# Routing the four-expert layer of a GNN/FFN kernel: dense blocks against blocks of one expert

## What is computed

```python
scores = _layernorm(agg, ln_gamma, ln_beta).reshape(M, HEADS, NUM_EXPERTS).mean(1)
...
topk_s, topk_i = jax.lax.top_k(scores, TOP_K)      # NUM_EXPERTS 4, TOP_K 2
w = jax.nn.softmax(topk_s, axis=-1)
out = jnp.zeros_like(x)
for ei in range(NUM_EXPERTS):
    g = jnp.where(topk_i == ei, w, 0.0).sum(-1)
    hh = jax.nn.gelu(x @ W1[ei] + b1[ei], approximate=False)
    out = out + g[..., None] * (hh @ W2[ei] + b2[ei])
```

## Time and profile before

| | |
|---|---|
| time, median of 3 runs | 7084.68 us (7082.7 to 7098.25) |
| the profiled execution | 7081.49 us, its span 7079.7 us |
| mean granted TensorE clock | 0.769 of full speed |
| busy: PE / DVE / POOL / ACT | 64% / 51% / 47% / 30% |
| dense experts of the fourth layer | from 4369 to 4742 us, 5% of the span |

### The profile page before, as it was taken

How to read it: one execution, slowest core, us unless ns; L and a number is a source line. 1 busy time by engine, 2 the same in 40 slices (tenths; PEclk the granted TensorE clock), 3 DMA queues, 4 the chain that set the end, 5 groups by cost and what they waited for, 6 DMA issues and landing times. The chain is left out here.

```text
span 7079.7 us, 66653 instructions
## 1 busy us (share of the span) xinstructions
PE 4547.3 (64%) x16642; PEld 3250.9 (46%) x16642; DVE 3616.6 (51%) x7881; ACT 2114.6 (30%) x4578; POOL 3328.5 (47%) x3063
## 2 busy tenths in 40 slices
PE   7699665569447880245545676985886774656373
PEld 3466444457336660112234343764665663334352
DVE  3344467631356666469734786226666125553422
ACT  4488300012123321155422112222332113554221
POOL 0677777624527770125410562005775134775045
PEclk9799867779766665679977898996666786676697
DMA  5233533346435552124420221004553444665054
GB/s 166 84 115 115 101 99 102 80 123 200 118 93 144 143 135 48 40 74 132 119 53 3 46 46 32 13 7 111 145 144 98 143 143 132 190 190 129 22 163 137
DMA packets 548714, 740.02 MB, mean 105 GB/s; under 512 B 191141, under 2 KB 405808, under 8 KB 545167
## 3 DMA queue, kind: packets, MB, share of 16 engines
q1 hardware_dynamic: 383920, 387.30, 19.8%
q0 software_dynamic: 164528, 349.77, 17.9%
HBM read 596.14 MB, written 143.55 MB: 104 GB/s over the span
## 5 line engine op out<-in xcount | busy, mean ns | idle before, releaser
L586 PE MATMUL ps<-msg,same 128*125 128x256 f32 (+2 forms) x3328 | 1387.1, 582 | 700.1 <-DMA msg<-rel_rows,src_rel 242.9
L586 PEld LDWEIGHTS ps<-msg,same 128*125 128x125 f32 x3328 | 865.5, 281 | 1053.3 <-DVE msg L680 304.2
L562 POOL DMA_INDIRECT msg<-d_gat,src_i x832 | 922.8, 1109 | 266.0 <-issue 242.2
L562 POOL DMA_INDIRECT msg<-d_lin,src_i x416 | 448.0, 1077 | 206.9 <-issue 124.9
L562 POOL DMA_INDIRECT msg<-rel_rows,src_rel x416 | 424.0, 1019 | 141.1 <-issue 118.8
L476 POOL DMA_INDIRECT rec<-rec,slot_i x391 | 421.8, 1079 | 119.1 <-issue 117.3
L573 PEld LDWEIGHTS ps_v<-vt,pick 125*128 125x128 f32 x1664 | 323.0, 273 | 173.2 <-issue 142.9
L618 ACT ACTIVATE off<-ramp_r,minus_lo 128x125 f32<-128x125 f32 x1248 | 390.6, 384 | 10.6 <-PEq L58 10.6
L412 PE MATMUL ps_f<-w,hs 128*128 128x256 f32 x1568 | 369.0, 389 | 35.4 <-DVE hs L451 35.4
L1213 ACT ACTIVATE hid<-ps_h,b 128x250 f32<-128x250 f32 x348 | 163.6, 470 | 718.7 <-PE ps_h L1178 718.3
L573 PE MATMUL ps_v<-vt,pick 125*128 x1664 | 290.7, 307 | 125.3 <-DVE pick L663 121.5
(11 more groups left out here) (556 smaller groups left out, 9157.8 us busy)
## 6 DMA issues: line engine op xcount, KB each, us to landing
lo_rows<-lo_r SPq DMA_DIRECT2D x208, 256.0 KB, 3.5
fil<-rec SPq DMA_DIRECT2D x104, 512.0 KB, 3.7
rows<-bc_d SPq DMA_DIRECT2D x96, 447.0 KB
w<-in_L_ffn_w SPq DMA_DIRECT2D x80, 512.0 KB
w<-in_L_ffn_w SPq DMA_DIRECT2D x32, 1024.0 KB
rel_rows<-row SPq DMA_DIRECT2D x25, 896.0 KB
answered<-y POOLq DMA_DIRECT2D x86, 224.0 KB
lo_rows<-ffn_lo_r SPq DMA_DIRECT2D x64, 250.0 KB
```

Of the source, the lines that this page charges most:

```text
L562: nc.gpsimd.indirect_dma_start(msg[:, g % R, j, :], None, table, bass.IndirectOffsetOnAxis(idx[:, n:n + 1], 0)).then_inc(msg_in[g % R], 16)
L586: nc.tensor.matmul(ps[:, j, 0:width], same[:, g % 2, j, :], msg[:, g % R, j, 0:width], start=True, stop=True).then_inc(mm, 1)
```

## The change

The dense stage goes. The fourth layer takes the form of `routed`, written out in `build` since its gates come from the attention: `project` also stores the normalised rows to `k.tokens`, `gates` gives `choice`, and `route`, `block_experts` and `fetch_rows` follow. With 2 of 4 experts chosen there are (6250 + 4 x 249) // 250 = 28 blocks. `fetch_rows` has neither `norm` nor `clean` nor `out`. No helper is changed.

```diff
-            with sbt("gate_i", [P, NT, 4]) as gate, sbt("cols_i", [128, 2, N]) as cols:
-                with sbt("rows_i") as rows:
-                    normalise_all(k, rows, cols)
-                with sbt("h16", [P, NT, 16]) as h16, sbt("agg_i", [P, NT, 20]) as agg, sbt("score_i", [P, NT, 4]) as score:
-                    project(k, cols, a["L1_ffn_W_gat"], 16, rows=h16, table=d["small"])
...
-                    gates(k, cols, gate, 4, None, None, "top2", scores=score[:])
-                experts(k, cols, gate, k.x, Experts(4, 512, ACT.Gelu, a["L1_ffn_W1"], a["L1_ffn_b1"], a["L1_ffn_W2"], a["L1_ffn_b2"]))
+            ex = Experts(4, 512, ACT.Gelu, a["L1_ffn_W1"], a["L1_ffn_b1"], a["L1_ffn_W2"], a["L1_ffn_b2"])
+            blocks = most_blocks(2, 4)
+            answered = k.answered[0:(blocks + 1) * BR, :]
...
+                with sbt("oh_i", [P, 2, NT, 4]) as oh:
+                    with sbt("rows_i") as rows, sbt("cols_i", [128, 2, N]) as cols:
+                        normalise_all(k, rows, cols)
...
+                            project(k, cols, a["L1_ffn_W_gat"], 16, rows=h16, table=d["small"], also=[(k.tokens.rearrange("(t p) f -> p t f", p=P), rows[:])])
...
+                            gates(k, cols, None, 4, None, None, "top2", scores=score[:], choice=(oh, wt))
+                    route(k, (oh, wt), slot_i, block_i, token_i, 4, 2, blocks)
+                block_experts(k, k.tokens, token_i, answered, block_i, ex, blocks)
+                fetch_rows(k, answered, slot_i, wt, 2, None)
```

More of the change, by code:

```diff
@@ new lines, in build @@
+            blocks = most_blocks(2, 4)
+            answered = k.answered[0:(blocks + 1) * BR, :]
+            with sbt("wt_i", [P, 2, NT]) as wt, sbt("slot_ii", [P, 2, NT], I32) as slot_i, sbt("token_ii", [P, 2 * blocks + 2], I32) as token_i, \
+                    sbt("block_ii", [1, blocks], I32) as block_i:
+                with sbt("oh_i", [P, 2, NT, 4]) as oh:
+                    with sbt("rows_i") as rows, sbt("cols_i", [128, 2, N]) as cols:
+                        normalise_all(k, rows, cols)
+                        with sbt("h16", [P, NT, 16]) as h16, sbt("agg_i", [P, NT, 20]) as agg, sbt("score_i", [P, NT, 4]) as score:
+                            project(k, cols, a["L1_ffn_W_gat"], 16, rows=h16, table=d["small"], also=[(k.tokens.rearrange("(t p) f -> p t f", p=P), rows[:])])
+                            scores(k, h16, 16, 4, a["L1_ffn_att_src"], a["L1_ffn_att_dst"], d["small"].rearrange("(t p) f -> p t f", p=P)[:, :, 16:20], tgt4, top4)
+                            small_edge_sums(k, d["small"], tgt4, top4, agg, a["ffn_src_c"], a["ffn_dst_c"])
+                            divide(k, agg, h16, 4, 1e-16, bias=a["L1_ffn_b_gat"], width=16)
+                            finish_norm(k, h16, None, a["L1_ffn_ln_gamma"], a["L1_ffn_ln_beta"], to_x=False, width=16)
+                            mean_heads(k, h16, score)
+                            gates(k, cols, None, 4, None, None, "top2", scores=score[:], choice=(oh, wt))
+                    route(k, (oh, wt), slot_i, block_i, token_i, 4, 2, blocks)
+                block_experts(k, k.tokens, token_i, answered, block_i, ex, blocks)
+                fetch_rows(k, answered, slot_i, wt, 2, None)
```

## The result

| | before | after |
|---|---|---|
| median of the runs, us | 7086.66 (7077.49 to 7101.24, 20 runs) | 7104.32 (7094.21 to 7116.14, 20 runs) |
| ratio | | 1.0025, 95% interval 1.0018 to 1.0032 |
| span of the profiled execution, us | 7079.7 | 7096.1 |
| from the end of `gates` to the next layer, us | 373.85 | 383.76 |

The change makes the kernel 17.7 us slower, just beyond the 0.2% (14 us) up to which the prediction called two times the same. The time, 7104.3, lies in the range of 7077 to 7110; the forecast was 7092.9 and +8.2, "same" its likeliest case. What came is the slower case, to which it had given 0.28, and what has to be explained is the 9.5 us between +8.2 and +17.7.

The account below looks back on a forecast made before the run. PE's full-clock matmuls were taken to bound the dense stage (348.66 of 373 us). Routed, 37.1 + 257.3 + 81.2 = 375.6 replaces 373.85, +1.75; with -0.2 and +6.65, +8.2 us, so 7084.68 becomes 7092.9, range 7077 to 7110.

Parts of the forecast that it names:

- the slower case: Whole kernel: slower than before by more than 14 us (0.2%), chance 0.28.
- gates, route, fetch: Fourth layer: gates -0.2 us; route 37.1, priced from the eighth layer; fetch 81.2 with 0.9 to the next layer.
- The table loads: Fourth layer's blocks: Gelu's 1.28 us activation table loads lie beside the matmuls, priced at nothing.
- project: Fourth layer: two token-store DMAs ahead of SP's 50 table stores add 6.65 us, bounds +3.7 and +10.
- I take the twin as it is: Fourth layer's block_experts: 28 blocks priced at 257.3 us from the second layer's block_experts, period 8.525 us.
- on the path whole: Fourth layer's blocks: load and block are level, so each tenth a load is longer adds fully to the path.
- 7.74 + 1.70: Fourth layer's blocks: highest period, PE's 7.74 us plus a 1.70 stop, giving at most 282 us for 28 blocks.
- Rival A: Fourth layer's blocks: weights later from rereading four megabytes and fewer empty slots; from 8.75 us a block; chance 0.26.
- The other layers: Later layers' stages: taken as unchanged; longer by more than a few us would show the prediction wrong.
- its +1.75: Fourth layer from gates to the next layer: route, blocks and fetch sum to 375.6 us in place of 373.85.
- The rule weighed: Blocks: a skill-page estimate puts a period's 1.75 MB at 6.0 us, under PE's 7.74, so no weight waits.
- rival B: Fourth layer's blocks: weights never late, periods fall to 7.74 us, kernel 7071.7 or 7069; chance 0.08.

Follow-up runs that it names:

- swap_func: Changed kernel with Relu and Gelu exchanged between the second and fourth layers' experts; 7105.87 us.
- early4: Changed kernel, fourth layer's blocks only: w1 and b1 of block n + 2 issued when block n's hidden layer is done; 7270.32 us, ratio 0.9981.
- early_all: Changed kernel with w1 and b1 of block n+2 issued once block n has read them, in all four routed layers; 7218.3 us, ratio 0.9909.
- again: The changed kernel once more, unaltered, for a second profile; 7117.64 us.
- bias_first: Changed kernel with the broadcast b2 issued first of a block's four DMAs instead of last, in the fourth layer; 7318.4 us, ratio 1.005.
- store_moved: Changed kernel with the token store taken out of project and issued by ACT at the head of small_edge_sums; 7306.44 us, ratio 1.003.

## Why the prediction was right, and where it wasn't

*gates, route, fetch.* -0.2 for -0.2; 37.3 for 37.1; 81.1 for 81.2 with the step to the next layer. Twins in the same trace priced these to a few tenths.

*The table loads* cost nothing, as said: 14 of them, each ended by the weights' DMA, and swap_func moves none of the time.

*project.* The right term, mis-sized: +8.3, in its bounds of 3.7 to 10. 3.2 of it is the later start of the 50 stores (6.08 us after SP's first DMA, before 2.93), which isn't made up, as said; the other 5.1 is that the stores behind the 3.2 MB take longer (26.73 less 21.66), which the sum had only inside the twin's total.

*block_experts.* The step that failed is "I take the twin as it is". Its period was taken at 8.525 and came at 8.803, +7.5 us, past the 8.75 that the prediction had named as a sign of being wrong. The working had said why it could: load and block are level. But its price for a late load, "on the path whole", was wrong in two ways. First, a stop gives the next load its time: in both stages, wherever PE waited from the third block on, the time from issue to use less this block's stop and the one before it is 7.1 to 7.5 us. A load later by a tenth then costs half of that a block, and 7.74 + 1.70 can't be every period. Where PE waited, the loads had taken 8.42 us in the twin and 8.69 here, in the mean; that is an estimated 0.13 us a block. Second, the clock: behind the stop of 2.37 the matmuls take 5.33 us, behind that of 1.70 in the twin they don't slow down. So a load later by 0.7 us cost 2.4, and nearly half of the 7.5 us (2 x 1.7, 0.13 a period) are two such falls.

*Rival A* came true with its outcome (it set its point at 8.75 us, and 8.80 gives 7100, +15.7 of the 17.7 with the rest of the sum) and fell with both of its reasons. Why the weights come later in this stage than in the second layer's is open. The table's function, the weights' addresses and the rows fetched don't account for it. Long periods stand at the same places in every run of the changed form with the old order of DMAs (the 4th, 6th, 18th, 20th and 22nd are 9.48 to 11.55 us), and half of the excess or more is in the first eight, which speaks for something fixed in the program or in where its tiles lie. The twin has such places too (its 23rd and 25th are 9.18 us or more in nine of ten traces), so that this doesn't set the stages apart, and no run here tells more.

*The other layers.* I had said unchanged. The eighth's blocks took 261.6 us (6749.91 to 7011.54) against 256.8 in the one trace of before, and 16.1 to 16.8 us a pair in the nine runs of kernels with the old issue order there against 16.0; `small_edge_sums` had +1.3, the stages between -2.1, those ahead of `project` -5.1. With the early issue the eighth layer's pair is the same, routed or dense (15.04 and 15.09), so what may have been given there lay in the waits for weights too. A single trace of before can't say more.

Added up by spans: 8.3 + 1.3 - 0.2 + 9.9 (the layer) - 5.1 - 2.1 + 4.9 - 0.6 = 16.4 us, the difference of 7096.1 and 7079.7. The layer is 8.1 over its +1.75 and `project` 1.65 over its term. The other stretches, which the sum had at nothing, moved by 0.6 to 5.1 each and cancel to -1.6; that they do so is luck and no part of the forecast.

*The rule weighed.* By the estimate from the Trainium skill, "DMA: Bandwidth & Descriptors", section "Anatomy of one DMA — SWDGE (gpsimd) path", a period's bytes take 6.0 us and no load would be late. The trace disagrees again, with 9.46 us from first issue to use; but in early4 and early_all, where half the load is issued earlier, the period is what rival B computed from PE's pace.

## What to carry to other kernels

When a load and the work that should hide it are equally long, a twin's period is not a price to build on: a few tenths decide, and the longest stops cost the clock as well. Look then at what the load waits for before asking what the load costs: here half of its bytes could be issued 4 us earlier, which was worth 1.2% in all, over four times what the change itself moved, and with it the routed form is the faster one. A store that nobody waits for still delayed what was issued behind or beside it, in each of the three places tried.

## What the runs showed of the hardware

- Over the block stages of the second, fourth and eighth layer in all fourteen traces, without each stage's first block: PE's stops of up to 1.85 us ahead of the first matrix's matmuls were followed by full clock. Of those from 1.86 us (`again`) to 2.90 some were and some were not (2.67 and 2.77 in `bias_first` were; 2.32 and 2.37 in the changed kernel were not). All beyond 3.0 us, 3.03 in `bias_first` the shortest, were followed by the lower clock. Where it fell, the 16 matmuls took 5.33 us in place of 3.6 in all but one case (6.57 behind 3.78, `store_moved`).
- The order of four DMAs on one queue is worth half a us a block (8.80 to 9.337, `bias_first`).
- 1.03 MB of weights with gathers and stores beside them took 7.5 to 9.5 us from first issue to use where PE waited for them (the second layer's stage before, the new stage after). In the load read in slices the bulk went through in 4 us, at 235 to 372 GB/s.
- The kernel before took 7079.56 us on the chip of the first experiments and 7282.49 and 7279.84 on the two later ones, 2.8% more, while the second layer's period with the old issue order was 8.49 to 8.60 us on all of them.
